# A three-layer macaron block on eight cores: four load slots for the second expert matrix, and Q/K projections read out of PSUM bank by bank

## The chip, the cores and the metric

The program runs on all 8 cores of one Trainium2 chip, cores 0 to 3 on one die and 4 to 7 on the other. Every core computes one batch element of 8 and exchanges nothing with the others. The time is device microseconds of the slowest core. TensorE's clock is granted at one of two levels, 1.2 or 2.4 GHz; the profile gives it as a share of 2.4 GHz.

## The reference

Input x is 8 x 2048 x 1024, float32 throughout. Three layers, each with a layernorm and a residual:

```python
x = x + 0.5 * ffn(layernorm(x))
x = x + attn(layernorm(x))
x = x + 0.5 * ffn(layernorm(x))

# ffn: groups of 32 tokens, 32 experts x 4 sets = 128 expert sets (es)
logits = einsum('bgtd,des->bgtes', grouped, controller) + tie
perm = (logits == max(logits, over t))             # one token of a group per es
dispatched = einsum('bgtd,bgtes->bgesd', grouped, perm)
inner = relu(einsum('bgesd,desf->bgesf', dispatched, f1) + bias)   # f: 32
intermediate = einsum('bgesf,esfd->bgesd', inner, f2)              # f2[es]: 32 x 1024
out = einsum('bgesd,bgtes->bgtd', intermediate, perm)

# attn: 16 heads of 64
Q, K, V = proj(x, Wq), proj(x, Wk), proj(x, Wv)
scores = (Q @ K.T + Q . rel_table[clip(i - j + 1023, 0, 2046)]) / 8
out = proj(softmax(scores) @ V, Wo)
```

## The kernel before

Every instruction is written out by hand into one list per engine (class Bld: wait, op, dma), so each engine and each DMA queue runs its list in program order, and waits are semaphore counts. A wait stands ahead of the next instruction of the same engine and holds everything behind it. One big SBUF tensor SCR is cut by column offsets (GTT, XA, HBASE, TAIL and offsets from them). PSUM is P0 (five banks of 512 columns), P1 (two) and P2 (one). A float32 matmul of the program is two MATMUL instructions in the trace.

emit_ffn runs twice, before and after emit_attn. After the routing logits it clears padding (lines 363 to 371): some SBUF regions are read with all 128 partitions though only the first 32 hold data, so partitions 32 to 127 are set to zero by two memsets for each region, and TensorE waits for the last of them. Then come four phases (gh 0 and 1, grp 0 and 1). A phase has a dispatch part (transposes of line 447, matmuls of line 464), in which TensorE gathers the chosen tokens, and then an expert part: 16 iterations over c, each with four expert sets. In an iteration TensorE does, in this order, emit_f1(c) (32 small matmuls, line 515), and emit_tail(c-1): four transposes (line 571), which VectorE copies to SBUF (line 582), then four f2 steps e4 = 0 to 3. An f2 step is two matmuls 128x32 by 128x512 (line 600, four MATMUL instructions) with one f2 matrix of 32 x 1024 from SBUF. Its result, 32 x 1024 in two banks of P0, is copied by ScalarE (line 615) to one of two SBUF buffers (ITS2), and GpSimd's queue stores that to DRAM (tensor itb). Behind the tail follows emit_bias(c) on VectorE (lines 540 and 553).

The f2 matrices are loaded on SyncE's queue into two slots (load_f2): the load of step j goes to slot j % 2 and waits until TensorE has finished step j - 2. Steps that use the same P0 half and the same ITS2 buffer are two apart too: ScalarE waits for the store of step j - 2 to land (semaphores iwa, iwb), and TensorE waits for ScalarE's copy of step j - 2. f1 matrices, 512 KB for each iteration, are loaded on the same queue (load_f1), two iterations ahead. In phase gh 0, grp 1 the queue also brings eight 512 KB tiles of the stored activations back (tensor hsc), issued between the dispatch and the expert part.

emit_attn works on 8 pairs of heads. For each pair the three weight slices are loaded, and then Q and K are projected: for Q and K, and for each head of the pair, 4 column blocks (nb) of 8 matmuls each (line 778) fill P0[0:64, 0:2048], four banks. One ScalarE instruction with the bias (line 790) copies all four banks to SBUF, and TensorE waits for it before it writes P0 again. So there are four such blocks in a pair, 64 MATMUL instructions in each; behind the last one TensorE goes on to V (line 807, into P1). The attention over 32 (head, query block) steps follows. It uses the relative-position table, which lies in SCR columns GTT to GTT + 4094 and is loaded again at the start of emit_attn. In emit_ffn that region is partly in use by f1's second slot (GTT to GTT + 1151).

Of the kernel before, what the change touches and what calls it, by code (L numbers as in the profile page):

```python
# [9 lines left out]
AF = mybir.ActivationFunctionType  # L10
# [54 lines left out]
def build_nc():  # L65
# [29 lines left out]
    with ExitStack() as stack:  # L95
# [4 lines left out]
        P0 = stack.enter_context(nc.psum_tensor("P0", [128, 2560], F32))  # L100
# [1 line left out]
        P2 = stack.enter_context(nc.psum_tensor("P2", [128, 512], F32))  # L102

        b = Bld(nc, stack)
        for s_ in ("ld", "sx", "so", "fla", "flb", "fba", "fbb", "gm",
                   "qwa", "qwb", "qwc", "gra", "grb", "grc",
                   "iwa", "iwb", "rha", "rhb", "xta", "xtb", "aow",
                   "hw", "hr", "lxa", "lxb", "lxc", "lxd", "rga", "rgb",
                   "pe", "ac", "ve"):
            b.sem(s_)  # L110
        DMA_SEMS = ("ld", "sx", "so", "fla", "flb", "fba", "fbb", "qwa", "qwb", "qwc",
                    "gra", "grb", "grc", "iwa", "iwb", "rha", "rhb",
                    "xta", "xtb", "aow", "hw", "hr", "lxa", "lxb", "lxc", "lxd",
                    "rga", "rgb")
# [5 lines left out]
        def scr(lo, hi, p0=0, p1=128):  # L120
            return SCR[p0:p1, lo:hi]

        GTT = 0
# [24 lines left out]
             inc="gm", n=1)  # L148
# [113 lines left out]
        def emit_ffn(src_hbm, dst_hbm, h_ve):  # L262
# [7 lines left out]
            F2BUF = XA + 11392  # L270
            F2B = XA + 14464
            ITS2 = XA + 12416
# [10 lines left out]
                      inc="ve")  # L283
# [78 lines left out]
            b.wait("vector", "ve", vperm_done)  # L362
            zpad = 0
            for (lo, hi) in ((STG, STG + 1024), (INT, INT + 512),
                             (F2BUF, F2BUF + 1024), (F2B, F2B + 1024)):
                for (p0, p1) in ((32, 64), (64, 128)):
                    zpad = b.op("vector",
                                lambda e, lo=lo, hi=hi, p0=p0, p1=p1: e.memset(
                                    scr(lo, hi, p0, p1), 0.0),
                                inc="ve", n=1)  # L370
# [5 lines left out]
            vb_prev = 0  # L376
            gp_prev_it = [0, 0]
            dve = b.cnt["ve"]
            F2S = (F2BUF, F2B)
            F2SEM = ("fba", "fbb")  # L380
            es_seq = [64 * grp_ + 4 * c_ + e4_
                      for gh_ in range(2) for grp_ in range(2)
                      for c_ in range(16) for e4_ in range(4)]
            f2_rd = [0, 0]
            f2_ld = [0, 0]
            ac_hist = [0] * (len(es_seq) + 2)
            f2_idx = 0

            def load_f2(j):
                if j >= len(es_seq):  # L390
                    return
                slot = j % 2
                b.wait("sync", "pe", f2_rd[slot])
                f2_ld[slot] = b.dma(
                    "sync", scr(F2S[slot], F2S[slot] + 1024, 0, 32),
                    f2r[32 * es_seq[j]:32 * es_seq[j] + 32, :], F2SEM[slot])

# [30 lines left out]
            b.wait("sync", "ve", h_ve)  # L428
            load_f2(0)
            load_f2(1)  # L430
            load_f1(0)
            load_f1(1)
            hr_ld = [0] * 8
            b.wait("vector", "hw", b.cnt["hw"])
            for gh in range(2):
                for grp in range(2):
# [127 lines left out]
                    def emit_tail(st):  # L564
                        nonlocal vT_prev, f2_idx
                        cb = st["cb"]
                        b.wait("tensor", "ve", st["vf1"])
                        b.wait("tensor", "ve", vT_prev)
                        for e4 in range(4):
                            b.op("tensor",  # L570
                                 lambda e, e4=e4, c=cb: e.matmul(
                                     P2[0:32, 128 * e4:128 * (e4 + 1)],
                                     SCR[0:128, STG + 128 * c + 32 * e4:
                                         STG + 128 * c + 32 * (e4 + 1)],
                                     IDENT[:, :], start=(e4 == 0),
                                     stop=(e4 == 3),
                                     is_transpose=True),
                                 inc="pe")
                        peT = b.cnt["pe"]
                        b.wait("vector", "pe", peT)  # L580
                        vT = b.op("vector",
                                  lambda e: e.tensor_copy(
                                      SCR[0:32, INT:INT + 512],
                                      P2[0:32, 0:512]),
                                  inc="ve")
                        vT_prev = vT
                        for e4 in range(4):
                            es = st["es0"] + e4
                            slot = f2_idx % 2
                            iw = "iwa" if slot == 0 else "iwb"  # L590
                            pb = 1024 * slot
                            b.wait("tensor", F2SEM[slot], f2_ld[slot])
                            if e4 == 0:
                                b.wait("tensor", "ve", vT)
                            if f2_idx >= 2:
                                b.wait("tensor", "ac", ac_hist[f2_idx - 2])
                            for bk in range(2):
                                b.op("tensor",
                                     lambda e, e4=e4, bk=bk, pb=pb,
                                     fo=F2S[slot]: e.matmul(  # L600
                                         P0[0:32, pb + 512 * bk:
                                            pb + 512 * (bk + 1)],
                                         SCR[0:128, INT + 128 * e4:
                                             INT + 128 * e4 + 32],
                                         scr(fo + 512 * bk,
                                             fo + 512 * (bk + 1), 0, 128),
                                         start=True, stop=True),
                                     inc="pe")
                            pef2 = b.cnt["pe"]
                            f2_rd[slot] = pef2  # L610
                            load_f2(f2_idx + 2)
                            b.wait("scalar", "pe", pef2)
                            b.wait("scalar", iw, gp_prev_it[slot])
                            acv = b.op("scalar",
                                       lambda e, slot=slot, pb=pb: e.activation(  # L615
                                           scr(ITS2 + 1024 * slot,
                                               ITS2 + 1024 * slot + 1024,
                                               0, 32),
                                           P0[0:32, pb:pb + 1024], AF.Copy,
                                           scale=1.0),  # L620
                                       inc="ac")
                            ac_hist[f2_idx] = acv
                            b.wait("gpsimd", "ac", acv)
                            gp_prev_it[slot] = b.dma(
                                "gpsimd",
                                itb[64 * es + 32 * gh:
                                    64 * es + 32 * gh + 32, :],
                                scr(ITS2 + 1024 * slot,
                                    ITS2 + 1024 * slot + 1024, 0, 32),
                                iw)  # L630
                            f2_idx += 1

# [90 lines left out]
        def emit_attn(src_hbm, dst_hbm, hfm_ve):  # L723
# [35 lines left out]
            for p in range(NPAIR):  # L759
# [10 lines left out]
                b.wait("tensor", "ac", b.cnt["ac"])  # L770
                b.wait("tensor", "ve", b.cnt["ve"])

                for (dst, wof, bof) in ((QF, 0, BQ), (KF, 1, BK)):
                    for hh in range(2):
                        for nb in range(4):
                            for m in range(8):
                                b.op("tensor",
                                     lambda e, wof=wof, hh=hh, nb=nb, m=m: e.matmul(  # L778
# [5 lines left out]
                                             HBASE + 2048 * m + 512 * (nb + 1)),  # L784
                                         start=(m == 0), stop=(m == 7)),
                                     inc="pe")
                        peq = b.cnt["pe"]
                        b.wait("scalar", "pe", peq)
                        aq = b.op("scalar",
                                  lambda e, dst=dst, bof=bof, p=p, hh=hh: e.activation(  # L790
                                      scr(dst + 2048 * hh, dst + 2048 * (hh + 1),
                                          0, 64),
                                      P0[0:64, 0:2048],
                                      AF.Identity,
                                      bias=scr(bof + p, bof + p + 1,
                                               64 * hh, 64 * (hh + 1)),
                                      scale=1.0),
                                  inc="ac")
                        b.wait("tensor", "ac", aq)
                b.wait("tensor", "gm", gp_ones)  # L800
                vev_hist = [0] * NT
                for c in range(NT):
# [408 lines left out]
```

How the kernel before makes its waits and increments, by code:

```python
    def wait(self, eng, semname, val):  # L45
        if val is None or val <= 0:
            return
        s = self.sems[semname]
        self.th[eng].append(lambda e, s=s, v=val: e.wait_ge(s, v))
# [1 line left out]
    def op(self, eng, fn, inc=None, n=1):  # L51
        if inc is None:
            self.th[eng].append(fn)
            return None
        self.cnt[inc] += n
        s = self.sems[inc]
        self.th[eng].append(lambda e, fn=fn, s=s, n=n: fn(e).then_inc(s, n))
        return self.cnt[inc]
```

## Time and profile before

| | |
|---|---|
| median of 3 runs | 9238.61 us (9202.23 to 9591.8) |
| profiled execution | 9221.16 us |
| span of its slowest core, core 0 | 9219.3 us |
| spans of cores 0 to 3 / 4 to 7, medians | 9212.4 / 9168.0 us |
| busy on core 0: TensorE, VectorE, ScalarE, GpSimd | 85%, 19%, 18%, 6% |
| DMA over the span | 104 GB/s |

The profile is of core 0. Busy time is the sum of an engine's instructions; matmuls overlap each other, and their ends are modelled. "Idle before" is the time that an engine did nothing before an instruction, with what ended it. A timeline row gives start, duration, engine, line, and how many equal instructions were merged into it.

### The profile page before, as it was taken

The numbers are of one execution on the slowest core, as the hardware profiler recorded it, in microseconds if no ns is written. First come the engines' busy times: TensorE is split into PE (matmuls) and PEld (weight loads), VectorE is DVE, ScalarE is ACT, GpSimd is POOL, SyncE is SP. The second block draws the span as 40 slices with busy tenths as digits, with TensorE's granted clock in tenths as the row PEclk, the third lists the DMA queues.
The fourth block names the chain that finished last, engine by engine and source line by source line (L and its number), as shares of the span: only waits on it lengthen the run. The fifth ranks groups of instructions, "written<-read, shape, count | busy, mean of one in ns | idle before, by whom it ended". The sixth has DMA issues, their size and how long they took to land.

```text
span 9219.3 us, 108855 instructions; the slowest of 8 cores (9151.6 to 9219.3 us)
## 1 busy us (share of the span) xinstructions
PE 7799.6 (85%) x44416; PEld 5239.9 (57%) x44416; DVE 1744.5 (19%) x3527; ACT 1683.5 (18%) x1415; POOL 571.3 (6%) x1096
## 2 busy tenths in 40 slices
PE   4888887479989899899899899899997857888886
PEld 3664562237747657567577477477476336446542
DVE  3221120112202202112112122022022132112110
ACT  0112112002202212112122022022122000221120
POOL 0001001000000000000000000000000000110010
PEclk7779769789989999999999999899898866887797
DMA  2224215604314314224134144043144120331236
GB/s 77 56 56 130 69 53 147 213 18 157 139 45 156 120 67 155 92 94 155 65 123 155 36 148 158 31 153 130 54 155 164 54 75 22 90 113 54 74 104 220
DMA packets 342582, 962.90 MB, mean 104 GB/s; under 512 B 38096, under 2 KB 198096, under 8 KB 275280
## 3 DMA queue, kind: packets, MB, share of 16 engines
q1 hardware_dynamic: 263248, 578.38, 18.2%
q0 software_dynamic: 78848, 377.56, 12.3%
q8 instruction: 364, 5.96, 0.3%
q14 instruction: 122, 1.00, 0.0%
HBM read 561.65 MB, written 394.13 MB: 104 GB/s over the span
## 4 chain that ended last, share of the span: by engine, by line
PE 81%; DMA 8%; DVE 6%; issue 3%; ACT 2%; SPq 1%; DVEq 0%; ACTq 0%; POOLq 0%
PE P L924 11%; PE P L960 11%; PE P L856 11%; PE P L778 10%; PE P L464 10%; PE P L600 8%; PE P L913 6%; DMA SCR<-f2r 3%; PE P L515 3%; PE P L1071 3%; PE P L807 3%; PE P L695 2%; DMA SCR<-itb 1%; PE P L305 1%; DVE SCR L975 1%
## 5 line engine op out<-in xcount | busy, mean ns | idle before, releaser
L600 PE MATMUL P<-SCR 128*32 128x512 f32 x2048 | 938.0, 594 | 269.9 <-DMA SCR<-f2r 124.6
L960 PEld LDWEIGHTS P<-SCR 128*128 128x128 f32 x8192 | 998.6, 203 | 251.4 <-issue 251.4
L960 PE MATMUL P<-SCR 128*128 128x128 f32 x8192 | 1046.7, 289 | 65.7 <-ACT SCR L944 65.7
L856 PE MATMUL P<-SCR 64*128 64x512 f32 (+1 forms) x2560 | 1061.1, 562 | 35.6 <-ACT SCR L871 35.6
L924 PE MATMUL P<-SCR 64*128 64x128 f32 x8192 | 1076.6, 283 | 0.0
L924 PEld LDWEIGHTS P<-SCR 64*128 64x128 f32 x8192 | 976.9, 192 | 88.6 <-issue 88.6
L778 PE MATMUL P<-SCR 128*64 128x512 f32 x2048 | 927.5, 615 | 117.8 <-DMA SCR<-wvt 64.9
L615 ACT ACTIVATE SCR<-P 32x1024 f32<-32x1024 f32 x512 | 518.0, 1012 | 2480.1 <-PE P L600 2296.7
L944 ACT ACTIVATE SCR<-SCR 128x1024 f32<-128x1024 f32 x512 | 541.1, 1057 | 2313.8 <-DVE SCR L935 2300.0
L464 PE MATMUL P<-SCR 128*128 128x64 f32 x4096 | 882.8, 419 | 60.4 <-DVE SCR L457 60.4
L464 PEld LDWEIGHTS P<-SCR 128*128 128x128 f32 x4096 | 872.6, 330 | 83.4 <-issue 83.4
L935 DVE COPY SCR<-P 128x1024 f32<-128x1024 f32 x512 | 627.1, 1225 | 1232.7 <-PE P L924 1227.5
L600 PEld LDWEIGHTS P<-SCR 128*32 128x32 f32 x2048 | 196.4, 109 | 931.3 <-issue 930.6
L778 PEld LDWEIGHTS P<-SCR 128*64 128x64 f32 x2048 | 287.6, 142 | 752.5 <-issue 752.5
L856 PEld LDWEIGHTS P<-SCR 64*128 64x128 f32 x2560 | 449.4, 200 | 463.3 <-issue 462.2
L913 PE MATMUL P<-IDENT,SCR 128*128 128x128 f32 x4096 | 552.6, 279 | 135.7 <-DVE SCR L975 135.7
L871 ACT ACTIVATE SCR<-P 128x2175 f32<-128x2175 f32 x256 | 507.5, 1983 | 720.1 <-PE P L856 713.7
L913 PEld LDWEIGHTS P<-IDENT,SCR 128*128 128x128 f32 x4096 | 461.8, 143 | 189.6 <-issue 189.6
L61 POOL DMA_DIRECT2D itb<-SCR x512 | 250.9, 490 | 3193.5 <-ACT SCR L615 2883.1
L695 PE MATMUL P<-SCR 128*128 128x512 f32 x512 | 278.7, 707 | 186.3 <-DMA SCR<-itb 166.0
L61 POOL DMA_DIRECT2D SCR<-qsl x256 | 141.5, 553 | 4209.1 <-PE P L924 2006.6
L478 DVE COPY SCR<-P 128x512 f32<-128x512 f32 x256 | 262.3, 1025 | 701.4 <-PE P L464 701.4
(61 smaller groups left out, 3435.2 us busy)
## 6 DMA issues: line engine op xcount, KB each, us to landing
qsl<-SCR SPq DMA_DIRECT2D x256, 1087.5 KB, 4.6
SCR<-qsl POOLq DMA_DIRECT2D x256, 1024.0 KB, 5.2
SCR<-f2r SPq DMA_DIRECT2D x512, 128.0 KB, 2.4
SCR<-f1r SPq DMA_DIRECT2D x128, 512.0 KB, 4.2
itb<-SCR POOLq DMA_DIRECT2D x512, 128.0 KB, 2.7
SCR<-itb POOLq DMA_DIRECT2D x64, 512.0 KB, 7.2
SCR<-itb SPq DMA_DIRECT2D x64, 512.0 KB, 5.7
xs<-SCR SPq DMA_DIRECT2D x32, 512.0 KB, 4.6
```

Source lines behind the costliest of these rows:

```text
L464: lambda e, hb=hb, m=m, a=a, grp=grp: e.matmul(P0[:, 256 * m + 64 * a: 256 * m + 64 * (a + 1)], scr(hb + 128 * m, hb + 128 * (m + 1)), scr ...
L600: fo=F2S[slot]: e.matmul(P0[0:32, pb + 512 * bk: pb + 512 * (bk + 1)], SCR[0:128, INT + 128 * e4: INT + 128 * e4 + 32], scr(fo + 512 * bk, ...
L615: lambda e, slot=slot, pb=pb: e.activation(scr(ITS2 + 1024 * slot, ITS2 + 1024 * slot + 1024, 0, 32), P0[0:32, pb:pb + 1024], AF.Copy, sca ...
L695: lambda e, t=t, a=a, bk=bk: e.matmul(P1[:, 512 * bk:512 * (bk + 1)], scr(PRMP + 512 * t + 128 * a, PRMP + 512 * t + 128 * (a + 1)), SCR[: ...
L778: lambda e, wof=wof, hh=hh, nb=nb, m=m: e.matmul(P0[0:64, 512 * nb:512 * (nb + 1)], scr(WSL + 1024 * wof + 128 * m + 64 * hh, WSL + 1024 * ...
L856: lambda e, h=h, q=q, o=o, wd=wd, w0=w0: e.matmul(P0[:, o:o + wd], SCR[0:64, QF + 2048 * h + 128 * q: QF + 2048 * h + 128 * (q + 1)], SCR[ ...
L871: lambda e, i=i: e.activation(SCR[:, sqr_off(i):sqr_off(i) + QW], P0[:, 0:QW], AF.Copy, scale=1.0),
L913: lambda e, i=i, kc=kc, j=j, PS=PS: e.matmul(PS[:, 128 * j:128 * (j + 1)], SCR[:, SPOS + 2048 * (i % 3) + 128 * kc: SPOS + 2048 * (i % 3) ...
L924: lambda e, h=h, q=q, kc=kc, j=j, PS=PS: e.matmul(PS[:, 128 * j:128 * (j + 1)], SCR[0:64, KF + 2048 * h + 128 * kc: KF + 2048 * h + 128 * ...
L935: lambda e, hf=hf, PS=PS: e.tensor_copy(SCR[:, ET + 1024 * hf: ET + 1024 * (hf + 1)], PS[:, 0:1024]),
L944: lambda e, hf=hf: e.activation(SCR[:, ET + 1024 * hf: ET + 1024 * (hf + 1)], SCR[:, ET + 1024 * hf: ET + 1024 * (hf + 1)], AF.Exp, scale= ...
L960: lambda e, voff=voff, kc=kc: e.matmul(P2[:, 0:128] if kc % 2 == 0 else P1[:, 0:128], SCR[:, ET + 128 * kc:ET + 128 * (kc + 1)], SCR[:, VS ...
```

## The change

1. The f2 matrices get four slots in place of two. The two new ones lie in the GTT region (GTT + 1152 to GTT + 3199), with semaphores fbc and fbd; the load of step j goes to slot j % 4 and waits for step j - 4. Four loads are issued ahead of the first step. P0 halves, ITS2 buffers and iwa/iwb still alternate over two (its2 = f2_idx % 2).
2. The padding of the two new slots is cleared too: four more memsets in emit_ffn.
3. In the Q/K projection every column block nb is copied out of its bank by a ScalarE instruction of its own (64 x 512), as soon as its 8 matmuls are done, and TensorE waits before block nb only for the previous copy of that bank. Behind the last block TensorE waits for all copies before V, as before.

```diff
             for (lo, hi) in ((STG, STG + 1024), (INT, INT + 512),
-                             (F2BUF, F2BUF + 1024), (F2B, F2B + 1024)):
+                             (F2BUF, F2BUF + 1024), (F2B, F2B + 1024),
+                             (GTT + 1152, GTT + 2176), (GTT + 2176, GTT + 3200)):
                 for (p0, p1) in ((32, 64), (64, 128)):
...
-            F2S = (F2BUF, F2B)
-            F2SEM = ("fba", "fbb")
+            F2S = (F2BUF, F2B, GTT + 1152, GTT + 2176)
+            F2SEM = ("fba", "fbb", "fbc", "fbd")
...
             def load_f2(j):
                 if j >= len(es_seq):
                     return
-                slot = j % 2
+                slot = j % 4
                 b.wait("sync", "pe", f2_rd[slot])
...
             load_f2(0)
             load_f2(1)
+            load_f2(2)
+            load_f2(3)
             load_f1(0)
...
-                            slot = f2_idx % 2
-                            iw = "iwa" if slot == 0 else "iwb"
-                            pb = 1024 * slot
+                            slot = f2_idx % 4
+                            its2 = f2_idx % 2
+                            iw = "iwa" if its2 == 0 else "iwb"
+                            pb = 1024 * its2
...
                             f2_rd[slot] = pef2
-                            load_f2(f2_idx + 2)
+                            load_f2(f2_idx + 4)
                             b.wait("scalar", "pe", pef2)
-                            b.wait("scalar", iw, gp_prev_it[slot])
+                            b.wait("scalar", iw, gp_prev_it[its2])
...
+                aq_nb = [0] * 4
                 for (dst, wof, bof) in ((QF, 0, BQ), (KF, 1, BK)):
                     for hh in range(2):
                         for nb in range(4):
+                            b.wait("tensor", "ac", aq_nb[nb])
                             for m in range(8):
...
-                        peq = b.cnt["pe"]
-                        b.wait("scalar", "pe", peq)
-                        aq = b.op("scalar",
-                                  lambda e, dst=dst, bof=bof, p=p, hh=hh: e.activation(
-                                      scr(dst + 2048 * hh, dst + 2048 * (hh + 1),
-                                          0, 64),
-                                      P0[0:64, 0:2048],
...
-                        b.wait("tensor", "ac", aq)
+                            peq = b.cnt["pe"]
+                            b.wait("scalar", "pe", peq)
+                            aq_nb[nb] = b.op(
+                                "scalar",
+                                lambda e, dst=dst, bof=bof, p=p, hh=hh,
+                                nb=nb: e.activation(
+                                    scr(dst + 2048 * hh + 512 * nb,
+                                        dst + 2048 * hh + 512 * (nb + 1),
+                                        0, 64),
+                                    P0[0:64, 512 * nb:512 * (nb + 1)],
...
+                b.wait("tensor", "ac", b.cnt["ac"])
                 b.wait("tensor", "gm", gp_ones)
```

## Rows read from the trace of the kernel before

**Rows 1.** Span and mean granted clock of core 0.
```profile
core 0: 9219.3 us, clock 0.869
```

**Rows 2.** The page's slices, 230 us each: granted TensorE clock in tenths.
```profile
PEclk7779769789989999999999999899898866887797
```

**Rows 3.** Waits of core 0: engine, line, awaited; us in total, times, longest.
```profile
PE P L600 <- DMA SCR<-f2r: 124.6, 135, 4.7
...
ACT SCR L615 <- DMA itb<-SCR: 81.6, 49, 2.8
...
PE P L778 <- ACT SCR L790: 52.9, 24, 2.2
...
PE P L807 <- ACT SCR L790: 18.5, 8, 2.3
```

**Rows 4.** Timeline of one expert iteration: start, us, engine, line, operation, count, idle before.
```profile
461.14 3.59 PE L600 MATMUL P<-SCR 128*32 128x512 f32 x8 [1.04 <-DVE SCR L540]
...
463.17 1.01 ACT L615 ACTIVATE SCR<-P 32x1024 f32<-32x1024 f32 x1 [4.47 <-PE P L600]
...
464.70 0.49 POOL L61 DMA_DIRECT2D itb<-SCR  x1 [4.99 <-ACT SCR L615]
...
465.62 3.81 PE L600 MATMUL P<-SCR 128*32 128x512 f32 x8 [0.89 <-DMA SCR<-f2r]
...
467.65 1.01 ACT L615 ACTIVATE SCR<-P 32x1024 f32<-32x1024 f32 x1 [1.76 <-DMA itb<-SCR]
...
469.27 2.19 PE L515 MATMUL P<-SCR 128*32 128x32 f32 x64
...
473.04 2.31 PE L600 MATMUL P<-SCR 128*32 128x512 f32 x5 [1.04 <-DVE SCR L540]
```

**Rows 5.** First and last tail of the first expert part, timeline.
```profile
366.66 3.59 PE L600 MATMUL P<-SCR 128*32 128x512 f32 x8 [0.93 <-DVE SCR L540]
...
542.63 3.59 PE L600 MATMUL P<-SCR 128*32 128x512 f32 x8 [1.04 <-DVE SCR L582]
```

**Rows 6.** Issue to landing, us: loads of f2r (whole span), then stores of itb (359 to 555 us).
```profile
DMA to landing us min/median/max: 2.0/2.4/7.6
...
DMA to landing us min/median/max: 2.1/2.7/4.5
```

**Rows 7.** Second phase, after the reload of hsc, timeline.
```profile
709.70 5.29 PE L600 MATMUL P<-SCR 128*32 128x512 f32 x8 [4.71 <-DMA SCR<-f2r]
```

**Rows 8.** Padding memsets and the first matmul behind them, timeline.
```profile
7650.16 0.91 DVE L368 MEMSET SCR<- 64x1024 f32 x1 [0.27 <-issue]
7651.34 0.91 DVE L368 MEMSET SCR<- 32x1024 f32 x1 [0.27 <-issue]
...
7653.79 1.09 PE L447 MATMUL P<-IDENT,SCR 128*128 128x128 f32 x4 [10.37 <-DVE SCR L368]
```

**Rows 9.** Q/K projection of the first pair and the start of V, timeline.
```profile
1935.33 29.35 PE L778 MATMUL P<-SCR 128*64 128x512 f32 x64 [2.21 <-ACT SCR L790]
...
1964.78 1.96 ACT L790 ACTIVATE SCR<-P,SCR 64x2048 f32<-64x2048 f32 x1 [29.59 <-PE P L778]
...
1966.88 27.65 PE L778 MATMUL P<-SCR 128*64 128x512 f32 x64 [2.20 <-ACT SCR L790]
...
2028.40 11.85 PE L807 MATMUL P<-SCR 128*128 128x128 f32 x104 [2.31 <-ACT SCR L790]
```

**Rows 10.** Windows, TensorE: stretch, us, busy (count), granted clock, DMA share, GB/s.
```profile
1935.00:1938.00 3.00, 2.67 (x4) 0.63 0.02 5
1938.00:1941.00 3.00, 3.00 (x7) 0.80 0.00 0
...
1967.00:1994.00 27.00, 27.00 (x64) 1.00 0.00 0
```

**Rows 11.** Windows: a dispatch and an expert part; PE, PEld, DVE, ACT, POOL, clock, DMA, GB/s.
```profile
893.00:1030.00 137.00, 119.57 (x578) 115.73 (x579) 37.97 (x40) 0.00 (x0) 0.00 (x0) 0.51 0.01 2
1030.00:1222.00 192.00, 158.13 (x1315) 63.70 (x1312) 20.67 (x97) 64.68 (x64) 31.21 (x64) 1.00 0.48 133
```

More of the change, by code:

```diff
@@ L104, in build_nc @@
         b = Bld(nc, stack)
-        for s_ in ("ld", "sx", "so", "fla", "flb", "fba", "fbb", "gm",
-                   "qwa", "qwb", "qwc", "gra", "grb", "grc",
+        for s_ in ("ld", "sx", "so", "fla", "flb", "fba", "fbb", "fbc", "fbd",
+                   "gm", "qwa", "qwb", "qwc", "gra", "grb", "grc",
                    "iwa", "iwb", "rha", "rhb", "xta", "xtb", "aow",
@@ L110, in build_nc @@
             b.sem(s_)
-        DMA_SEMS = ("ld", "sx", "so", "fla", "flb", "fba", "fbb", "qwa", "qwb", "qwc",
+        DMA_SEMS = ("ld", "sx", "so", "fla", "flb", "fba", "fbb", "fbc", "fbd",
+                    "qwa", "qwb", "qwc",
                     "gra", "grb", "grc", "iwa", "iwb", "rha", "rhb",
@@ L383, in emit_ffn @@
                       for c_ in range(16) for e4_ in range(4)]
-            f2_rd = [0, 0]
-            f2_ld = [0, 0]
+            f2_rd = [0, 0, 0, 0]
+            f2_ld = [0, 0, 0, 0]
             ac_hist = [0] * (len(es_seq) + 2)
@@ L610, in emit_tail @@
                             f2_rd[slot] = pef2
-                            load_f2(f2_idx + 2)
+                            load_f2(f2_idx + 4)
                             b.wait("scalar", "pe", pef2)
-                            b.wait("scalar", iw, gp_prev_it[slot])
+                            b.wait("scalar", iw, gp_prev_it[its2])
                             acv = b.op("scalar",
-                                       lambda e, slot=slot, pb=pb: e.activation(
-                                           scr(ITS2 + 1024 * slot,
-                                               ITS2 + 1024 * slot + 1024,
+                                       lambda e, its2=its2, pb=pb: e.activation(
+                                           scr(ITS2 + 1024 * its2,
+                                               ITS2 + 1024 * its2 + 1024,
                                                0, 32),
@@ L623, in emit_tail @@
                             b.wait("gpsimd", "ac", acv)
-                            gp_prev_it[slot] = b.dma(
+                            gp_prev_it[its2] = b.dma(
                                 "gpsimd",
@@ L627, in emit_tail @@
                                     64 * es + 32 * gh + 32, :],
-                                scr(ITS2 + 1024 * slot,
-                                    ITS2 + 1024 * slot + 1024, 0, 32),
+                                scr(ITS2 + 1024 * its2,
+                                    ITS2 + 1024 * its2 + 1024, 0, 32),
                                 iw)
@@ L786, in emit_attn @@
                                      inc="pe")
-                        peq = b.cnt["pe"]
-                        b.wait("scalar", "pe", peq)
-                        aq = b.op("scalar",
-                                  lambda e, dst=dst, bof=bof, p=p, hh=hh: e.activation(
-                                      scr(dst + 2048 * hh, dst + 2048 * (hh + 1),
-                                          0, 64),
-                                      P0[0:64, 0:2048],
[L794 to L798, printed above, removed]
-                        b.wait("tensor", "ac", aq)
+                            peq = b.cnt["pe"]
[8 more added lines that the diff above has]
+                                    P0[0:64, 512 * nb:512 * (nb + 1)],
+                                    AF.Identity,
+                                    bias=scr(bof + p, bof + p + 1,
+                                             64 * hh, 64 * (hh + 1)),
+                                    scale=1.0),
+                                inc="ac")
+                b.wait("tensor", "ac", b.cnt["ac"])
                 b.wait("tensor", "gm", gp_ones)
```

## The prediction

> **What bounds the kernel now.** Look first at the span of the slowest core [rows 1]: 9219.3 us, at a mean granted clock of 0.869. Each of the two expert-layer runs and the attention is a string of TensorE work in program order, so time is won where TensorE stands still, or where its clock comes up. Then look at the waits [rows 3] for the two kinds of idle time that the change addresses. TensorE waited 124.6 us, 135 times, for loads of f2 ahead of line 600, and 52.9 + 18.5 us, 24 + 8 times, for ScalarE's copy of the Q/K banks. Both are plain stalls on TensorE's own path. ScalarE has little to do, but its copies in the expert part waited 81.6 us for stores of itb to land; this chain is kept as it is, so I follow it below.
>
> The wait totals understate the first stall. The timeline of one iteration [rows 4] shows what an iteration is made of. TensorE starts the tail's f2 steps at 461.14, stops after eight MATMULs for the third load (0.89 us idle by the record), starts again at 465.62, goes to f1 at 469.27 and begins the next tail at 473.04. So the f2 steps take 8.13 us and the rest 3.77 us. The rows of the projection give the pitch of such a matmul without any wait: 64 in 27.65 us, 0.43 us each [rows 9]. Sixteen of them are 6.9 us. The load costs 1.2 us in this iteration, not 0.89, because the modelled end of a matmul lies behind its pitch and gaps between single matmuls are not counted.
>
> **The change, part by part.**
>
> *Four f2 slots.* SyncE now issues the load of step j + 4 when step j is done. The step that needs it comes one whole iteration later, over 10 us, while a load takes 2.4 us (longest 7.6) [rows 6]; with two slots it came one step later, 1.7 us. An iteration becomes 6.9 + 3.77 = 10.65 us. An expert part has 15 intervals between first f2 steps of its 16 tails; the last one has no f1 work and is 2.0 us shorter. That makes 14 x 10.65 + 8.65 = 157.8 us, and 1262 us for eight parts. Before it is 175.97 us in the first part [rows 5]; the eight spans, each read as in these rows, lie between 175.4 and 181.2 us and add up to 1422 us. The difference is 160 us.
>
> What is late next? Follow ScalarE and the stores [rows 4]. Copy of step 0 at 463.17, 1.01 us long, store issued at 464.70, landed by 467.65 when the copy of step 2 starts: 4.48 us from copy to copy on one ITS2 buffer. Two of these are 9.0 us, under the new period by 1.7 us, with 2.7 us as the median landing. The longest landing in this stretch is 4.5 us [rows 6]. The fourth store of an iteration is issued beside the 512 KB f1 load and is likely the slow one; for it the margin is about 1 us, and TensorE has 0.3 us more, since it waits for the copy two steps back. I take 0.15 us for each of 112 intervals for stores that come late, 17 us; the bounds are nothing and, if every landing were 4.5 us, 2 x (1.01 + 0.52 + 4.5) = 12.1 us an iteration, no gain at all. I stay close to the lower end because the median row is. In two of the eight parts the reload of hsc makes the third step wait 4.71 us [rows 7], and the first interval is 17.2 us. Four resident slots take the f2 loads out of that, but the f1 load queued behind the same 4 MB is then what TensorE reaches first, so I give back 3.5 us of this. Left: 160 - 17 - 3.5 = 140 us. Behind the last tail of a part I count no gain, since the next dispatch waits for the last copy, hence for the store chain.
>
> On SyncE's queue nothing is moved past anything else: each f2 load stays where it stood and waits for the same step, only its slot is newer. f1 loads stay behind the fourth step, two iterations ahead.
>
> *Padding.* Two more regions, two memsets each, at a pitch of 7651.34 - 7650.16 = 1.18 us, and TensorE waits for the last of them [rows 8]: 4.7 us, twice, so 9.4 us lost.
>
> *Copies by bank.* One copy of 2048 columns took 1.96 us [rows 9], one of 1024 columns 1.01 us [rows 4], so 512 columns take about 0.54 us (bounds 0.49, a quarter of the first, and 1.01). A block of 16 MATMULs takes 6.9 us, and a bank is written again three blocks later, so all but the last copy of a pair are covered; even at 1.01 us they would be. Of the four stalls in a pair three vanish: from copy to copy the short ones take 29.85 us, against 64 x 0.43 = 27.5 without the wait. That is 2.35 x 24 = 56 us. The fourth, ahead of V, shrinks from 2.31 us by 1.96 - 0.54 = 1.42: 11 us over 8 pairs.
>
> There is a second gain in the clock. Of the 24 blocks behind such a stall some take 27.65 us and some 29.35 [rows 9]. The windows show why [rows 10]: right behind the stall that begins at 1933 us the granted clock is 0.63 and then 0.80, and in the block that took 27.65 us it is 1.00 throughout. From the starts of the 32 copies, 14 of the 24 intervals are the long kind (31.55 us) and 10 the short (29.85). A stall that brings the clock to its lower level for a while costs 1.70 us more; without the stalls I take all 14 back, 24 us (bounds 0 and 24). The first block of each pair, behind the weights' load, stays slow. If the short kind had been reached by chance and the falls came back elsewhere, the sum would be 24 us less, 198 us.
>
> **The sum.** 140 - 9.4 + 56 + 11 + 24 = 222 us. The profiled execution took 9221.16 us: 9221 - 222 = 8999 us, 2.4% less. That execution lies between the fastest run (9202) and the median (9239) of the three, so the same gain makes 8980 to 9017 from those.
>
> **The rivals.**
>
> *The store chain takes the place of the load.* If landings grow to some 4.3 us because the same bytes now move in 10% less time, the iteration is 2 x (1.01 + 0.52 + 4.3) = 11.66 us, 0.2 below the 11.86 of before. The expert parts give 22 us and not 140; the total is 22 - 9 + 91 = 104 us: 9117 us. For it: ScalarE already waited for stores 49 times [rows 3], and the fourth store is the slow one. Against it: median 2.7 us [rows 6], and the DMA share in an expert part is only 0.48 [rows 11].
>
> *The clock falls in the fuller streams, and the kernel gets slower.* The lengthened streams are 128 x 6.9 + 8 x 110 = 1760 us of matmuls at 2.4 GHz. They must run at a mean clock of 1760 / (1760 + 222) = 0.89 to lose all that is gained. The attention stretches show 8 and 9 tenths [rows 2], and the dispatch parts, busy for 87% of the time, 0.51 [rows 11]; so a busy TensorE alone doesn't hold the clock up. At 0.85 the loss is 311 us and the time 9310. Against it: a whole expert part with 82% busy stood at 1.00 [rows 11], and 27 us without any gap stood at 1.00 [rows 10]. The Trainium skill (TensorE: Matmul & The Clock Gate, section Seeing it yourself) warns of a limiter that holds a die at 13/16 of the full clock when most of its cores run dense matmuls; by it the streams would cost 1760 x (16/13 - 1) = 406 us more and the time would be 9405. The 27 us at 1.00, with all cores in the same stage, speak against it here.
>
> *Only the projection pays.* The f2 load was the last to arrive but something else comes within tenths of it, such as TensorE's wait for the copy two steps back: copy of step 0 ends at 464.18, and the third step could start at 461.14 + 3.44 = 464.58, 0.4 us later. If that wait takes half of the 1.2 us, the gain is 70 - 9 + 91 = 152 us: 9069 us.
>
> **How the numbers follow.** My forecast (gain 185 to 250 us) has 0.69. Rival one, including halfway cases, 0.14; rival three 0.11; the falling clock 0.06, of which 0.05 ends slower by over 2% or nearly so. The range 8955 to 9125 us takes in the forecast (its upper end is the whole 160 us, no late stores, against a fast run), rival three and rival one, and leaves out the falling clock and both tails. About 2% is what a measurement of this kernel can tell from no change, 184 us; the forecast passes it by only 38 us. Faster by over 2%: 0.70, the forecast and little else. Within 2%: 0.25. Slower: 0.05.
>
> **What would show it.** In the profile after: the wait of line 600 for f2r gone or under 15 us; 10.6 to 10.9 us between tails; ScalarE's waits for itb longer than 81.6 us, but TensorE's waits for ScalarE's copy at line 600 under 20 us; the wait at line 447 behind the memsets 4.7 us longer; 128 copies of 64x512 at about 0.54 us, no wait at line 778 for them; a granted clock of 1.00 behind the first block of each pair. A clock under 0.95 in an expert part, or a period over 11.3 us, would make the prediction wrong.

## The result and the profile after

| | before | after |
|---|---|---|
| median of 10 executions each | 9705.74 us (9202.23 to 9999.6) | 9144.26 us (8956.83 to 9517.92) |
| ratio, without the executions of which the next sentence speaks | | 0.9749 (95% interval 0.9696 to 0.9801) |

In more than half of the executions of either kernel one die or both ran at a lower granted clock and took some per cent longer, which is why both medians lie far above the lowest times; the ratio, and all readings below where nothing else is said, leave these executions or dies out. By the ratio the changed kernel is 2.5% faster (the interval runs from 2.0 to 3.0%), against the 2.4% of the forecast. The median of 9144 us lies 19 us above the upper end of the forecast range, 9125 us.

The profile after is that of the same kernel run again (the first experiment). Its die 1 stands at the mean granted clock that the kernel before had there. The view is the spans of the dies:

```profile
die 0 (median of its cores): 9550.3 us, clock 0.805
die 1 (median of its cores): 8946.7 us, clock 0.873
```

Die 1 of the kernel before took 9168.0 us at 0.874 (median of its cores), so at the same clock the change is worth 221 us. The rest is read on core 4 of this run, beside the rows of before, which are of core 0.

Waits, longest in total first (engine, line, awaited; us, times, longest), answering to [rows 3]; line numbers have moved, 605 is the f2 matmul, 620 its copy, 785 the Q/K matmul, 799 its copy, 817 V, 451 the first transposes of a dispatch part, 370 the padding:

```profile
ACT SCR L620 <- DMA itb<-SCR: 381.1, 180, 5.4
...
PE P L605 <- DVE SCR L544: 121.3, 117, 1.1
...
PE P L451 <- DVE SCR L370: 30.2, 2, 15.1
...
PE P L605 <- ACT SCR L620: 20.4, 22, 2.0
...
PE P L817 <- ACT SCR L799: 8.3, 8, 1.0
```

The wait of the f2 matmul for its load (124.6 us before) and that of the Q/K matmul for ScalarE (52.9 us) have no row any more. V waits 1.0 us in each pair and not 2.3. ScalarE's waits for stores rose from 81.6 to 381 us; TensorE's own waits for ScalarE's copies are 20.4 us in all. The padding holds the first transposes for 15.1 us in each expert layer, 4.7 more than the 10.37 of [rows 8].

An iteration of an expert part, timeline, answering to [rows 4]:

```profile
448.29 7.03 PE L605 MATMUL P<-SCR 128*32 128x512 f32 x16 [1.04 <-DVE SCR L544]
...
450.32 1.01 ACT L620 ACTIVATE SCR<-P 32x1024 f32<-32x1024 f32 x1 [2.14 <-PE P L605]
...
454.94 1.01 ACT L620 ACTIVATE SCR<-P 32x1024 f32<-32x1024 f32 x1 [1.90 <-DMA itb<-SCR]
455.15 2.19 PE L519 MATMUL P<-SCR 128*32 128x32 f32 x64
...
458.98 3.59 PE L605 MATMUL P<-SCR 128*32 128x512 f32 x8 [1.10 <-DVE SCR L544]
```

The sixteen MATMULs of a tail now run without a break, 448.29 to 455.15, 6.86 us, and the next tail begins 10.69 us after this one (11.9 before). ScalarE's copy of the third step starts at 454.94, when the store of the first step's result has landed; ScalarE stood idle for 1.9 us before it.

The first pair's projection, timeline, answering to [rows 9], and its window (stretch, us, busy and count of PE, PEld, DVE, ACT, POOL, clock, DMA share, GB/s), answering to [rows 10]:

```profile
1909.83 0.68 ACT L799 ACTIVATE SCR<-P,SCR 64x512 f32<-64x512 f32 x1 [6.19 <-PE P L785]
1916.69 0.68 ACT L799 ACTIVATE SCR<-P,SCR 64x512 f32<-64x512 f32 x1 [6.19 <-PE P L785]
1917.63 28.82 PE L817 MATMUL P<-SCR 128*128 128x128 f32 x256 [1.03 <-ACT SCR L799]
```
```profile
1815.70:1927.40 111.70, 110.67 (x323) 41.74 (x322) 1.78 (x10) 10.23 (x15) 0.00 (x0) 1.00 0.00 0
```

A copy comes every 6.87 us, each 0.68 us long, and TensorE waits for none but the last. The granted clock is 1.00 for 111.7 us on end, which takes in everything but the first 11 us of the pair's projection; the kernel before had 0.63 and 0.80 behind a stall [rows 10].

The stages by the first and last starts of their matmuls, in us (worked out from the traces):

| | before, mean of cores 4 to 7 | after, mean of cores 4 to 7 | difference | forecast |
|---|---|---|---|---|
| routing and padding, two layers | 287.1 | 295.9 | +8.8 | +9.4 |
| first to last f2 matmul, two layers | 2358.7 | 2216.1 | -143 | -140 |
| projections and attention, 8 pairs | 5243.4 | 5154.6 | -89 | -91 |

### The profile page after: what moved, and what is told of

It is laid out like the page before. It is cut to its first block, busy times and chain, and to the rows that moved or that the text cites. A ratio compares the mean times of both kernels' runs of the same rounds, so it can differ in the third digit from the quotient of the medians.

```text
span 9109.4 us, 109129 instructions; the slowest of 8 cores (9045.5 to 9109.4 us)
## 1 busy us (share of the span) xinstructions
PE 7863.5 (86%) x44416; PEld 5336.9 (59%) x44416; DVE 1750.1 (19%) x3535; ACT 1707.0 (19%) x1511; POOL 571.4 (6%) x1096
## 3 DMA queue, kind: packets, MB, share of 16 engines
q14 instruction: 123, 1.01, 0.0%
## 4 chain that ended last, share of the span: by engine, by line
PE 83%; DMA 6%; DVE 6%; issue 3%; ACT 1%; SPq 0%; DVEq 0%; ACTq 0%; POOLq 0%; POOL 0%
PE P L934 12%; PE P L970 12%; PE P L866 12%; PE P L785 10%; PE P L468 10%; PE P L605 8%; PE P L923 6%; PE P L519 3%; PE P L1081 3%; PE P L817 3%; PE P L700 2%; DMA itb<-SCR 2%; DMA SCR<-itb 2%; PE P L306 1%; DVE SCR L985 1%
## 5 line engine op out<-in xcount | busy, mean ns | idle before, releaser
L970 PEld LDWEIGHTS P<-SCR 128*128 128x128 f32 x8192 | 1026.2, 207 | 257.9 <-issue 257.9
L970 PE MATMUL P<-SCR 128*128 128x128 f32 x8192 | 1075.2, 294 | 65.8 <-ACT SCR L954 65.8
L866 PE MATMUL P<-SCR 64*128 64x512 f32 (+1 forms) x2560 | 1097.6, 578 | 35.6 <-ACT SCR L881 35.6
L934 PE MATMUL P<-SCR 64*128 64x128 f32 x8192 | 1106.8, 288 | 0.0
L934 PEld LDWEIGHTS P<-SCR 64*128 64x128 f32 x8192 | 1005.3, 197 | 91.7 <-issue 91.7
L605 PE MATMUL P<-SCR 128*32 128x512 f32 x2048 | 903.3, 592 | 147.4 <-DVE SCR L544 124.9
L468 PEld LDWEIGHTS P<-SCR 128*128 128x128 f32 x4096 | 872.8, 330 | 83.2 <-issue 83.2
L866 PEld LDWEIGHTS P<-SCR 64*128 64x128 f32 x2560 | 462.1, 205 | 481.8 <-issue 480.8
L985 DVE COPY SCR<-P 128x128 f32<-128x128 f32 x256 | 74.6, 291 | 1719.5 <-PE P L970 1719.5
```

The costliest lines, as they stand in the source:

```text
L468: lambda e, hb=hb, m=m, a=a, grp=grp: e.matmul(P0[:, 256 * m + 64 * a: 256 * m + 64 * (a + 1)], scr(hb + 128 * m, hb + 128 * (m + 1)), scr ...
L605: fo=F2S[slot]: e.matmul(P0[0:32, pb + 512 * bk: pb + 512 * (bk + 1)], SCR[0:128, INT + 128 * e4: INT + 128 * e4 + 32], scr(fo + 512 * bk, ...
L866: lambda e, h=h, q=q, o=o, wd=wd, w0=w0: e.matmul(P0[:, o:o + wd], SCR[0:64, QF + 2048 * h + 128 * q: QF + 2048 * h + 128 * (q + 1)], SCR[ ...
L934: lambda e, h=h, q=q, kc=kc, j=j, PS=PS: e.matmul(PS[:, 128 * j:128 * (j + 1)], SCR[0:64, KF + 2048 * h + 128 * kc: KF + 2048 * h + 128 * ...
L970: lambda e, voff=voff, kc=kc: e.matmul(P2[:, 0:128] if kc % 2 == 0 else P1[:, 0:128], SCR[:, ET + 128 * kc:ET + 128 * (kc + 1)], SCR[:, VS ...
```

## The experiments

Each kernel was run beside the kernel before on one chip; ratios are to it, with 95% intervals. For experiments 7 and 8 and for the repetition in experiment 6 there is no ratio, and they are read from their traces.

**1. The changed kernel again.** No edit.

> The changed kernel itself, for a profile whose cores stand at the clock of the profile before. Theory A (stalls removed, as forecast): 222 us less than before, ratio 0.976; 10.6 to 10.9 us between tails of an expert part, no wait of line 785 for ScalarE, clock 1.00 behind the first block of a pair. Theory B (the fuller streams pull the clock down by themselves): granted clock in the expert parts and in the Q/K blocks under 0.95 on a core of an undisturbed die, and a gain under 180 us.

Ratio 0.9746 (0.9700 to 0.9792). Between tails of an expert part core 4 shows 10.63 us in most intervals. The eight parts take 157.4, 159.9, 158.2, 160.3, 158.7, 162.3, 158.1 and 158.2 us from the transposes of the first tail to those of the last, 1273 together; on core 4 of the kernel before they take 1419: 146 us less, against the 140 of the forecast. The clock was 1.00 in the Q/K blocks and 0.97 in a window over an expert part and little else (1010 to 1170 us). Theory A holds on this die.

Die 0 of this same execution shows a lower clock, here over the attention (windows of core 2, then of core 4):

```profile
5000.00:6000.00 1000.00, 947.11 (x4868) 674.59 (x4867) 178.38 (x363) 210.44 (x161) 54.45 (x97) 0.82 0.30 111
...
5000.00:6000.00 1000.00, 943.06 (x5117) 639.48 (x5118) 174.10 (x374) 210.16 (x169) 50.87 (x91) 0.94 0.29 107
```

Same program, same share of busy time, 0.82 against 0.94. The clock records of the traces say what this is (the sums are worked out from them): besides the two levels of 1.0 and 0.5 they hold a third one, 0.8125 of 2.4 GHz. Core 2 spent 3934 of its 9583 us there and the other three cores of die 0 3579 to 3905 us; none of the four cores of die 1 was there at all. The time at 0.5 is nearly the same on all eight cores, 2253 to 2365 us. The kernel before has it too: 180 to 234 us on the four cores of die 0 in its profile, and an execution beside this one in which a die took 9955 us (median of its cores) at a mean clock of 0.79. So it is not the change's doing.

**2. Only the f2 slots and their padding.** emit_attn as before.

> Edits 1 and 2 alone (four f2 slots and their padding; the Q/K copies as before). Theory A: 131 us less than before, ratio 0.986. The store chain as the new bound: 13 us less, ratio 0.999, with ScalarE's waits for itb at some 1 us for every step. Only half of the f2 wait gained: 61 us less, 0.993.

Ratio 0.9838 (0.9770 to 0.9905): 149 us of 9200 (87 to 212), against 131. The two rival readings (13 and 61 us less) lie outside the interval, at 0.999 and 0.993. On core 5 ScalarE waited 383.4 us for stores and TensorE 17.6 us for ScalarE, as in the whole change: the store chain came forward but did not take over.

**3. Only the copies by bank.** emit_ffn as before.

> Edit 3 alone (Q/K copies by bank; two f2 slots as before). Theory A: 91 us less, ratio 0.990: 67 us of stalls and 24 us of clock. If the falls of the clock behind the stalls come back elsewhere: 67 us, 0.993. Together with the slots-only kernel the gains should add up to that of the whole change; a sum that is larger by over 20 us speaks for a clock that the two parts together lose.

Ratio 0.9908 (0.9855 to 0.9962): 85 us, against 91; the interval does not by itself exclude 67. The two parts' ratios multiply to 0.9747, the ratio of the whole: as far as these intervals tell, the gains add up. That the clock's share is in it is seen in the stage: from the first Q/K matmul to the first of the output projection it takes 5149 to 5156 us on the four cores of die 0, against 5240 to 5247 on cores 4 to 7 before, at least 83 us less, which the stalls alone (67) do not give. On these four cores all 24 blocks that follow another block of their pair are short.

**4. Padding on GpSimd.**

```diff
+            b.wait("gpsimd", "ve", h_ve)
+            for lo in (F2BUF, F2B, GTT + 1152, GTT + 2176):
+                for (p0, p1) in ((32, 64), (64, 128)):
+                    b.op("gpsimd",
+                         lambda e, lo=lo, p0=p0, p1=p1: e.memset(
+                             scr(lo, lo + 1024, p0, p1), 0.0),
+                         inc="gm", n=1)
+            pad_gm = b.cnt["gm"]
...
-                             (F2BUF, F2BUF + 1024), (F2B, F2B + 1024),
-                             (GTT + 1152, GTT + 2176), (GTT + 2176, GTT + 3200)):
```

> The changed kernel with the padding memsets of all four f2 slots moved from VectorE to GpSimd, at the start of emit_ffn, where GpSimd is idle. Theory A (the memsets lie on TensorE's path): the wait of the first dispatch transposes falls from 15.1 us to about 5.7 in each expert layer, 19 us less than the changed kernel, ratio to before 0.974. Rival (the memsets were covered, or GpSimd's own slow VectorE's copies in the routing part): no difference, or a routing part that is longer by as much.

Ratio 0.9748 (0.9680 to 0.9815), no difference from the changed kernel that can be measured. But the wait is shorter as forecast (waits of core 4; in the changed kernel 30.2 us in two):

```profile
PE P L459 <- DVE SCR L377: 11.5, 2, 5.8
```

and routing with padding takes 138.9 and 139.0 us on core 1, against 147.3 and 148.0 on core 4 in experiment 1: 17 us less where the edit is. Die 0, at 0.872 here, has a median of 8944.2 us against 8946.7. On core 1 the first layer's scatter part (itb read back) took most of it back, 214.2 us against 202.5; over the cores of the kernel before, of experiment 1 and of this one that part varies between 197 and 222 us. So the memsets do lie on TensorE's path, and 19 us are below what these executions resolve.

**5. Three f2 slots, three store buffers, padding on GpSimd.**

```diff
-            F2S = (F2BUF, F2B, GTT + 1152, GTT + 2176)
+            F2S = (F2BUF, F2B, GTT + 1152)
+            ITS2S = (ITS2, ITS2 + 1024, GTT + 2176)
+            IWS = ("iwa", "iwb", "fbd")
...
-                            slot = f2_idx % 4
-                            its2 = f2_idx % 2
+                            slot = f2_idx % 3
+                            its2 = f2_idx % 3
```

The matmul output still alternates over two halves of P0, and the queues that read itb back wait for all three semaphores.

> Three f2 slots and three ITS2 buffers (the store of a step has three steps to land, not two), padding of the f2 slots on GpSimd. If the late intervals of 11 to 12 us between tails are the store chain: they vanish, every interval is 10.63 us, 12 us less than the changed kernel, and with the padding some 30 us less; ScalarE's waits for itb near nothing. If they come from the f2 or f1 loads, they stay, and with three slots the wait for f2r may come back. The three slots alone should be enough for the loads: a load then has two steps, 3.4 us, against the 2.4 us of its median landing.

Ratio 0.9699 (0.9672 to 0.9726), some 45 us less than the changed kernel by the ratios, whose intervals overlap, and some 30 us less by the spans (medians of the dies 8917.9 and 8912.6 us, against 8946.7). ScalarE's and TensorE's waits on core 4:

```profile
PE P L615 <- DMA SCR<-f2r: 7.8, 5, 3.4
...
ACT SCR L630 <- DMA itb<-SCR: 4.2, 2, 2.7
```

The waits for stores fell from 381 to 4 us, TensorE's wait for ScalarE's copy has no row any more, and six of the eight parts on core 4 take 157.4 to 158.0 us. In the changed kernel 16 to 20 of the 112 full intervals on a core are over 10.75 us; here 4 to 8 are. So the late intervals were mostly the store chain. In the intervals it cost less than the 12 us expected: the six parts without a reload of hsc take 158.6 us from first to last tail in experiment 1 and 157.5 here (means of all cores), 1.1 us a part and 6 us in all, and the two parts behind a reload did not get shorter (324 us together in both). A second cost lies behind the last tail of a part, where the next dispatch waits for the last copy: from that tail's first f2 step to the dispatch it is 10.0 us in experiment 1 and 8.7 here, six times, so 8 us more. Three slots serve the loads as well as four, but for the 7.8 us of waits for f2r shown above.

**6. The transposes ahead of f1.** As experiment 5, and emit_tail is cut in two.

```diff
                     for c in range(16):
+                        if prev_st is not None:
+                            emit_tr(prev_st)
                         st = emit_f1(c)
                         if prev_st is not None:
                             emit_tail(prev_st)
```

> As the three-slot kernel, and the tail's four transposes stand ahead of f1 in TensorE's list, so that VectorE's copy of them (TensorE waited 124.9 us for it in the changed kernel, 1.04 us each) runs beside f1. If that wait is what ends last now: intervals of 9.6 us and not 10.63, 124 us less than the three-slot kernel, ratio to before about 0.958. If the store chain or the loads are close behind, less: at 4.5 us of store landing in each of three buffers the chain allows 2.0 us a step, 8.0 us an iteration, so it should not bind.

Ratio 0.9621 (0.9580 to 0.9662), 72 us less than experiment 5 by the ratios, not 124. The interval between tails is 9.55 us as forecast, in seven parts of eight on core 4. In the fourth part of core 4 it was 10.9 us, at this clock (window of core 4, TensorE only; core 5 of the same die reads 0.85):

```profile
1240.00:1300.00 60.00, 60.00 (x476) 0.86 0.53 142
```

while core 0 had 1.00 in the same window. By the clock records core 4 spent 125 of the 164 us of this part at 0.8125. Hence the repetition:

> The kernel with the transposes ahead of f1 once more, since its first profile shows one expert part on one die at a granted clock of 0.86 with 10.9 us between tails, against 9.55 us in the other parts. If that part was a disturbance of the die: eight parts at 9.55 us, spans of some 8790 to 8820 us, ratio to before 0.957. If this denser stream pulls the clock down by itself: parts at 10.9 us again, on cores of both dies, ratio 0.962 as before.

> The changed kernel once more beside it, for the difference on the same chip: 8950 to 8990 us, ratio to before 0.975; the kernel above is then 160 to 170 us faster than the changed one (124 from the order of the transposes, 19 from the padding, 12 to 15 from the third store buffer, and some of the reload stall).

In the second execution there is no such part: timeline of core 5,

```profile
443.69 2.21 PE L528 MATMUL P<-SCR 128*32 128x32 f32 x64
...
443.86 0.68 DVE L595 COPY SCR<-P 32x512 f32<-32x512 f32 x1 [6.55 <-PE P L584]
...
445.73 7.03 PE L620 MATMUL P<-SCR 128*32 128x512 f32 x16
...
453.24 2.21 PE L528 MATMUL P<-SCR 128*32 128x32 f32 x64
```

VectorE's copy now runs beside f1, the f2 matmuls start without a wait, and 453.24 - 443.69 = 9.55 us. The spans of all eight cores are 8784 to 8834 us; those of die 0 of the changed kernel beside it, at 0.873, are 8932 to 8973 us. The medians of these two groups of spans, 8809 and 8950, lie 141 us apart, less than the 160 to 170 expected. Some of the rest is seen: the two parts behind the reloads of hsc take 146 to 161 us from the transposes of the first tail to those of the last, not 144; TensorE waits 9 to 11 us for f2r (cores 0, 4 and 5; 7.8 in experiment 5); and the transposes of each part's first tail now wait 1.2 us for VectorE, 9.6 us in all, in place of 6.4 us ahead of f1. From first to last f2 step the eight parts take 1159 us against 1269 in experiment 5 (means of all cores), so the new order gave 111 us of the 124. The fall to 0.86 is the third level of experiment 1 again, since the clock records have no other level beside it and 1.0 in that part. Whether a denser stream makes it more frequent is neither shown nor excluded: in the profiled executions the cores spent nothing at 0.8125 in experiment 5, 237 to 632 us in experiment 6, and 0 to 150 us in its repetition. Its ratio of 0.962 is the lowest of the kernels here.

**7. and 8. How long a stall brings the clock down.** In the changed kernel, TensorE now waits for all copies ahead of each block of 64 MATMULs. The diff is that of experiment 7; in experiment 8 ScalarE also copies two banks at a time (64 x 1024), behind nb = 1 and nb = 3. The kernels were executed twice and once.

```diff
                     for hh in range(2):
+                        b.wait("tensor", "ac", max(aq_nb))
                         for nb in range(4):
-                            b.wait("tensor", "ac", aq_nb[nb])
```

> The changed kernel, but ahead of each block of 64 TensorE waits for all copies by bank, so a stall of about 0.9 us stands where the kernel before has 2.2 us. If any stall brings the clock down: blocks of 29.35 us behind some of them. If it takes a longer stall: all blocks 27.65 us, granted clock 1.00, and 24 x 0.9 = 22 us more than the changed kernel.

> As the one before with two copies of two banks each, so a stall of about 1.3 us. The same two readings: either blocks of 29.35 us appear (clock falls behind a stall of 1.3 us as behind 2.2), or all stay at 27.65 us and the fall needs more than 1.3 us.

Groups of the two kernels on core 4 (line, engine, operation, count, busy us, mean ns, idle before):

```profile
L785 PE MATMUL P<-SCR 128*64 128x512 f32 x2048 | 902.5, 602 | 87.0 <-DMA SCR<-wvt 64.8 <-ACT SCR L799 22.2
```
```profile
L785 PE MATMUL P<-SCR 128*64 128x512 f32 x2048 | 900.1, 601 | 99.1 <-DMA SCR<-wvt 66.7 <-ACT SCR L800 32.4
...
L800 ACT ACTIVATE SCR<-P,SCR 64x1024 f32<-64x1024 f32 x64 | 70.9, 1108 | 1060.3 <-PE P L785 1060.3
```

There are 24 stalls of 0.93 us in the first and 24 of 1.35 us in the second. None of them brought the clock down: across a stall the interval from copy to copy is 7.98 us in the first (6.87 without) and 15.27 in the second (13.74 without), and all 192 blocks behind a stall on the eight cores are of the short kind, in either run. In the kernel before, 14 of the 24 blocks behind the stalls of 2.2 us are long on core 0, and 107 of the 192 on all eight cores; in experiment 2, whose projection is that of before, 108 of 192. The stage from the first Q/K matmul to the output projection took 5179 and 5185 us (means of cores 4 to 7), 25 and 31 us more than in the changed kernel; by the rows above the stalls add up to 22 and 32 us. So the 24 us of clock were real, and they depended on the stall's length.

## Why the prediction was right, and what was off

**The path.** Both stalls lay on TensorE's own path, and 222 us were forecast from them. At equal clock it is 221 us between the medians of die 1 in the two profiles, and 2.5% by the ratio.

**The iteration.** 10.65 us were worked out from the pitch and from the 3.77 us of other work; 10.63 us were measured. Reading the wait's row alone (124.6 us) would have missed nearly a fifth: the eight parts became 146 us shorter, and late stores had taken 6 us of the gain.

**What is late next.** The store chain, as named. The forecast took 17 us off the intervals for it; experiment 5 puts it at 6. It had the wrong store for the slow one: not the fourth of an iteration but mostly the first and the third come late. On core 4 the third step's copy waits for a store 110 times in 128 iterations (191 us) and the first step's 41 times (144 us), the fourth step's 28 times (46 us), but the second step's, which needs the fourth store, once. TensorE's 20.4 us on core 4 are just over the 20 us that were named as the limit (13.8 on core 5). The rival in which the chain takes over fell with experiment 2.

**The reload.** The f1 load behind hsc was named as the next to be late, and on core 4 it is, once, for 0.77 us:

```profile
683.67 2.18 PE L519 MATMUL P<-SCR 128*32 128x32 f32 x64 [0.77 <-DMA SCR<-f1brep]
```

The two parts together take 322 us on cores 4 to 7, 7 us more than two parts at 157.5, where 3.5 had been given back.

**Padding.** 9.4 us forecast, 8.8 measured.

**The copies.** A copy of 512 columns takes 0.68 us, not 0.54. The straight line was drawn through two kinds of copy, one of the expert part (32 x 1024, 1.01 us, no bias) and one of the projection (64 x 2048, 1.96 us, with bias). The projection's own copies lie on a line, 0.68, 1.11 (experiment 8) and 1.96 us for 512, 1024 and 2048 columns, 0.10 us above the other kind at 1024. It is not the number of partitions, since ScalarE's instructions of 128 x 1024 take 1.04 to 1.06 us; whether it is the bias no run shows. The 0.14 us that were missing cost 1 us over the kernel. The wait ahead of V fell by 1.28 us and not 1.42.

**The clock behind the stalls.** All 24 us came back. That the falls come back elsewhere is excluded for the projection, since all 96 blocks behind another block are short on cores 4 to 7 (56 of 96 were long before), and for the attention behind it by the 89 us of the whole stage.

**Only the projection pays.** TensorE's wait for the copy two steps back was 20.4 us in all, where the rival wanted half of the 160.

**The step that failed is the range, through the term of the falling clock.** The range was built around one profiled execution, and its upper end of 9125 us came from the rivals' gains alone. The fall of the clock was left out of it: it had a chance of 0.06, and the forecast asked only whether the change would bring it. It comes without the change, and it adds more than the 19 us by which the time missed the range. The median of 9144.26 us lies halfway between two executions, 9111.0 and 9177.5 us, in which the slower die had a mean clock of 0.855 and 0.845. The first of them has a trace: by its clock records core 5 spent 967 of its 9109 us at 0.8125, and every other core 679 to 977 us. If work at that level takes 16/13 of its time, this is 967 x 3/16 = 181 us, and 9109 - 181 = 8928 us is close to what the cores of die 1 took in experiment 1 without it (8931 to 8971); this is an estimate from the records. The four executions of the changed kernel in which both dies had a mean clock of 0.865 or more took 8957 to 9025 us, all within the range. So the gain was right and the range for an absolute time too narrow by this term. The sign of it was in view: one of the three executions of before took 9591.8 us, and in the profile before itself the cores of die 0 had spent 180 to 234 us at 0.8125 and those of die 1 none, which by the same estimate is 34 to 44 us of the 44 between the dies (9212.4 and 9168.0). That TensorE's clock has two levels, as said at the top, is not the whole of it. Nor were the 27 us at 1.00 a reason against the limiter: core 0, on which they were read, spent 234 us at 0.8125 in other stretches.

The Trainium skill's limiter (TensorE: Matmul & The Clock Gate, section Seeing it yourself) holds a whole die at 13/16 of the full clock under dense matmuls. The trace agrees on the level, 0.8125 in the records, and on the whole die, four cores of die 0 alike (0.803 to 0.808 over the span). It does not agree that dense matmuls on all cores always bring it on: die 1 stood at 0.94 in the same stretch and was never at that level.

## What to carry to other kernels

An idle time put down to a load is only part of what the load costs when the engine before it is a pipelined TensorE: take the pitch of an unbroken stream and the distance between two equal points of the loop; here the price of an iteration came out within 0.02 us (10.65 forecast, 10.63 measured). When one of two resources that alternate over two buffers gets four, follow the other that stays at two; here its waits grew from 82 to 381 us, of which TensorE felt little, and a third buffer removed them. A stall can cost a fall of the clock besides its length: the stalls of 2.2 us did so here in over half of the cases, those of 0.93 and 1.35 us in none, so shortening a stall gave that part back without removing the stall. And before an absolute time is forecast, ask in how many executions the clock of a die falls whatever the kernel does; a ratio between executions at the same clock does not need that answer.

## What the runs showed of the hardware that I had not expected

- Behind a stall of 2.2 us TensorE's clock fell in 107 of 192 cases on the eight cores, for 1.70 us of added time each; behind stalls of 0.93 and of 1.35 us in none of 192.
- The clock records hold a third level, 0.8125, beside 0.5 and 1.0. In one execution all four cores of one die spent 3.6 to 3.9 ms there and the four of the other none, running the same program on the same amount of data; the spans differ by 600 us.
- Dispatch matmuls (128 columns of weights, 64 moving columns) run at the lower level of 1.2 GHz in both kernels, at 0.51 with TensorE 87% busy before [rows 11] and at 0.50 with 86% after (560 to 640 us, core 4 of experiment 1), and the expert part that follows in the same list at 1.00 and 0.97.
